# Summing the edge masks through four column quarters of the tensor engine, joined one row later, in a three-layer graph network kernel

## The reference, cut to what matters

```python
for l in range(N_LAYERS):                       # 3
    f1 = relu(x[row] @ nb_W[l] + nb_b[l]); f2 = relu(x[col] @ self_W[l] + self_b[l])
    h = relu(concatenate([f1, f2], axis=1) @ att1_W[l] + att1_b[l])
    log_alpha = (h @ att2_W[l] + att2_b[l])[:, 0]
    mask = clip(sigmoid(log_alpha) * (ZETA - GAMMA) + GAMMA, 0.0, 1.0)
    rowsum = segment_sum(mask, row, num_segments=n) + 1e-06
    d_inv_sqrt = clip(rowsum ** (-0.5), 0.0, 10.0)
    vals = mask * d_inv_sqrt[row] * d_inv_sqrt[col]
    x = segment_sum(vals[:, None] * x[col], row, num_segments=n)
    out = out + x
```

## Time and profile before

| what | before |
|---|---|
| median of 3 runs | 4434.0 us (4422.53, 4434.0, 4437.3) |
| the profiled execution's own time | 4420.38 us |
| its span in the profile | 4418.5 us |
| tensor engine matmul busy | 3818.8 us (86%) |
| tensor engine weight loads busy | 3641.2 us (82%) |
| vector engine busy | 3743.0 us (85%) |
| scalar engine busy | 1965.6 us (44%) |
| GpSimd busy | 2440.8 us (55%) |
| mean granted clock of the tensor engine | 0.947 of full speed |
| mask stage of layer 1, first to last matmul of the mask sums | 1350.7 to 1829.2 us |
| the same of layer 2 | 2392.9 to 2873.2 us |
| the same of layer 3 | 3437.9 to 3918.0 us |

### The profile page before, as it was taken

The page is one execution under the profiler, slowest core; times in us unless marked ns, Lnnn a source line. Parts: engine busy times, 40 slices in busy tenths (PEclk is TensorE's granted clock), DMA queues, the critical chain, the costliest instruction groups (busy, mean ns, idle before and its releaser), DMA issues. The chain is left out here.

```text
span 4418.5 us, 256510 instructions
## 1 busy us (share of the span) xinstructions
PE 3818.8 (86%) x99277; PEld 3641.2 (82%) x99278; DVE 3743.0 (85%) x5930; ACT 1965.6 (44%) x4794; POOL 2440.8 (55%) x3237
## 2 busy tenths in 40 slices
PE   5888577877859999799988999979997999979997
PEld 4777477777739999788886999979886999978887
DVE  8999878888867888799995888789996788879998
ACT  5888466776731212255552121145553112125554
POOL 3655377777831222388982222279885122238887
PEclk8888799999979999899998999989998999989999
DMA  1000099999926777566653777656662677756665
GB/s 30 2 2 2 17 268 285 294 286 283 287 68 233 243 243 244 165 171 171 171 141 128 242 244 242 215 156 171 170 171 82 222 243 244 243 159 171 172 171 138
DMA packets 533726, 794.14 MB, mean 180 GB/s; under 512 B 67990, under 2 KB 467786, under 8 KB 533642
## 3 DMA queue, kind: packets, MB, share of 16 engines
q1 hardware_dynamic: 500714, 714.25, 51.3%
q0 software_dynamic: 32928, 78.72, 8.3%
HBM read 672.34 MB, written 120.42 MB: 179 GB/s over the span
## 5 line engine op out<-in xcount | busy, mean ns | idle before, releaser
L1370 POOL TENSOR_TENSOR message<-message 128x448 f32<-128x448 f32 x1029 | 1242.4, 1239 | 211.1 <-ACT message L1354 211.1
L1141 PE MATMUL pre_ps<-rows_a,hotT_a 128*128 128x64 bf16 x21609 | 1289.8, 194 | 45.2 <-DMA hotT_a<-hot_scratch 27.9
L1141 PE MATMUL pre_ps<-table,hotT_a 128*128 128x64 bf16 x21609 | 1290.6, 194 | 7.1 <-issue 6.9
L1141 PEld LDWEIGHTS pre_ps<-rows_a,hotT_a 128*128 128x128 fp8e4 x21609 | 1132.2, 98 | 52.7 <-issue 52.3
L1141 PEld LDWEIGHTS pre_ps<-table,hotT_a 128*128 128x128 fp8e4 x21609 | 1132.9, 98 | 8.0 <-issue 8.0
L1381 DVE TENSOR_TENSOR message<-message 128x448 f32<-128x448 f32 x1029 | 993.7, 966 | 69.3 <-POOL message L1370 69.3
L1221 DVE SCALAR_TENSOR_TENSOR weighed<-pre_ps,w 128x448 f32<-128x448 f32 x1029 | 643.1, 625 | 311.0 <-PE pre_ps L1141 219.2
L1354 ACT ACTIVATE message<-high_ps,mask 128x64 f32<-128x64 f32 x3087 | 699.8, 327 | 295.2 <-PE high_ps L1313 276.5
L1325 PE MATMUL sum_ps<-message,hot_b 128*128 128x192 bf16 x7203 | 783.9, 247 | 6.3 <-DVE message L1381 5.7
L1313 PE MATMUL low_ps<-table,hot_b 128*128 128x64 bf16 x12348 | 531.5, 193 | 160.6 <-DMA hot_b<-hot_scratch 65.3
L1189 POOL TENSOR_SCALAR fresh<-gate 128x49 f32<-128x49 f32 x147 | 35.3, 240 | 1114.8 <-ACT gate L1169 1114.8
(11 more groups left out here) (150 smaller groups left out, 4988.0 us busy)
## 6 DMA issues: line engine op xcount, KB each, us to landing
hotT_a<-hot_scratch SPq DMA_DIRECT2D x1029, 224.0 KB, 4.5
hot_b<-hot_scratch SPq DMA_DIRECT2D x1029, 224.0 KB, 2.8
hot_scratch<-hot SPq DMA_DIRECT2D x343, 336.0 KB, 10.3
hot_a<-hot_scratch SPq DMA_DIRECT2D x147, 784.0 KB, 5.1
places<-slots_scratch POOLq DMA_DIRECT2D x686, 112.0 KB, 6.8
out<-res SPq DMA_DIRECT2D x1, 1536.0 KB
slots_scratch<-bins SPq DMA_DIRECT2D x49, 16.0 KB, 1.4
raw<-in_src SPq DMA_DIRECT2D x1, 768.0 KB
```

The costliest lines, as they stand in the source:

```text
L1141: last = nc.tensor.matmul(pre_ps[g][:, j, :], hotT[:, b, g, end, j * P:(j + 1) * P].bitcast(FP8), table, start=end + part == 0, stop=end = ...
L1370: pool.tensor_tensor(message[:, g, :, 1, :], message[:, g, :, 0, :], top[:, g, :, 0, :, 1], ALU.subtract).then_inc(s["rest_ready"], 1)
```

## The change

The roles of the two operands in the mask sums are swapped, and the 49 bins are dealt out over four column tiles of the array. The three parts of a bin's masks become the stationary operand (3 columns, at column 0, 32, 64 or 96 by the bin's number modulo 4) and the one-hot matrix becomes the moving one (128 columns). So each quarter of `total_ps[:, 0:128]` holds, in three of its partitions, sums over a quarter of the bins. The scalar engine copies the 128 x 128 result out twice (bf16 and f32), GpSimd splits it into three bf16 parts (three operations), and in the next row three matmuls with a column of ones add all partitions up into `total_ps[:, 128:129]`, after group 1. The vector engine copies this column out after group 2, in place of the reduction at the row's end. The mask sums stand after group 4 in place of group 5. The scalar engine now makes the gates first, copies the table rows of the next row after them, and then waits for the mask sums. The table gets a 50th, zeroed block so that this copy may run one row past the end. The sync engine waits for the mask sums (`quartered`) in place of `summed`. After the last row come one join, the last mask sums, their copy and split, and one more join.

```diff
-    SUMS_AT = max(0, NG - 2)
+    SUMS_AT = max(0, NG - 3)
+    ADD_AT = min(1, SUMS_AT)
@@ sync engine
-                    wait_count(sp, s, s["summed"], r + 1)
+                    wait_count(sp, s, s["quartered"], r + 1)
@@ tensor engine
                     pe.wait_ge(s["parts_ready"], r + 1)
-                    pe.wait_ge(s["taken"], r + 1)
+                    pe.wait_ge(s["taken"], r + 2)
...
-                            last = nc.tensor.matmul(total_ps[:, 0:PARTS], hot[:, b, g, j * P:(j + 1) * P].bitcast(FP8),
-                                                    parts[:, t, :], start=t == 0, stop=t == NB - 1)
+                            at = 32 * (t % 4)
+                            last = nc.tensor.matmul(total_ps[at:at + PARTS, 0:P], parts[:, t, :],
+                                                    hot[:, b, g, j * P:(j + 1) * P].bitcast(FP8), start=t < 4,
+                                                    stop=t >= NB - 4, tile_position=(0, at), skip_group_check=True)
+                    last.then_inc(s["quartered"], 1)
+
+                def add_quarters(next_but_one):
+                    pe.wait_ge(s["quarters_ready"], next_but_one)
+                    pe.wait_ge(s["taken"], next_but_one)
+                    hold_waits(pe, s)
+                    for part in range(PARTS):
+                        last = nc.tensor.matmul(total_ps[:, P:P + 1], quarter_parts[:, part, :], unit[:, :],
+                                                start=part == 0, stop=part == PARTS - 1)
                     last.then_inc(s["summed"], 1)
...
                         gather(r * NG + g, r, g, b, nth)
+                        if g == ADD_AT and not first:
+                            add_quarters(r)
                         if g == SUMS_AT and not first:
                             sum_masks(r - 1, 1 - b, nth if b == 1 else nth - 1)
                 each_row(pe, NB, row)
+                add_quarters(NB)
                 sum_masks(NB - 1, 0, NB // 2 + 1)
+                add_quarters(NB + 1)
@@ scalar engine
+                def take_quarters(r):
+                    act.wait_ge(s["quartered"], r + 3)
+                    act.wait_ge(s["summed"], r + 1)
+                    nc.scalar.activation(quarter_parts[:, 0, :], total_ps[:, 0:P], ACT.Copy)
+                    nc.scalar.activation(quarters[:, :], total_ps[:, 0:P], ACT.Copy).then_inc(s["quarters_taken"], 1)
...
                 def row(r, b, nth, first):
-                    if not first:
-                        act.wait_ge(s["gathered"], r * NG)
-                    nc.scalar.activation(rows[:, b, :].rearrange("p (a d) -> p a d", d=D),
-                                         k.table_s[:, bass.ds(r, 1), :, :].rearrange("p r a d -> p (r a) d"),
-                                         ACT.Copy).then_inc(s["rows_ready"], 1)
-                    if not first:
+                    if first:
+                        fetch_rows(0, 0)
+                        fetch_rows(1, 1)
+                    else:
                         gates(r - 1, 1 - b)
+                        act.wait_ge(s["gathered"], (r + 1) * NG)
+                        fetch_rows(r + 1, 1 - b)
+                        take_quarters(r - 1)
                 each_row(act, NB, row)
                 gates(NB - 1, 0)
+                take_quarters(NB - 1)
@@ GpSimd
                     pool.sem_inc(s["parts_ready"], 1)
+                    wait_count(pool, s, s["quarters_taken"], r + 1)
+                    step(pool.tensor_tensor(quarters[:, :], quarters[:, :], quarter_parts[:, 0, :], ALU.subtract))
+                    step(pool.tensor_copy(quarter_parts[:, 1, :], quarters[:, :]))
+                    step(pool.tensor_tensor(quarter_parts[:, 2, :], quarters[:, :], quarter_parts[:, 1, :], ALU.subtract))
+                    pool.sem_inc(s["quarters_ready"], 1)
@@ vector engine
                 dve.sem_inc(s["weigh"], NG)
-                dve.sem_inc(s["taken"], 1)
+                dve.memset(unit[:, :], 1.0)
+                dve.memset(quarter_parts[:, :, :], 0.0).then_inc(s["quarters_ready"], 1)
+                dve.memset(total_ps[:, 0:P], 0.0).then_inc(s["taken"], 1)
...
-                def take(r, b):
-                    dve.wait_ge(s["summed"], r + 3)
-                    dve.tensor_reduce(k.sums[:, bass.ds(r, 1)], total_ps[:, 0:PARTS], X, ALU.add).then_inc(s["taken"], 1)
+                def take(next_but_one):
+                    dve.wait_ge(s["summed"], next_but_one)
+                    dve.tensor_copy(k.sums_from[:, bass.ds(next_but_one - 1, 1)], total_ps[:, P:P + 1])\
+                        .then_inc(s["taken"], 1)
...
-                    if not first:
-                        take(r - 1, 1 - b)
+                        if g == ADD_AT + 1 and not first:
+                            take(r)
```

More of the change, by code:

```diff
@@ L146, in allocate @@
     k.one, k.two = k.both[:, :, 0:k.D], k.both[:, :, k.D:2 * k.D]
-    k.table = sb("table", [P, k.NB, PARTS, 2 * k.D], BF16)
+    k.table_all = sb("table", [P, k.NB + 1, PARTS, 2 * k.D], BF16)
+    k.table = k.table_all[:, 0:k.NB, :, :]
     k.table_s, k.table_d = k.table[:, :, :, 0:k.D], k.table[:, :, :, k.D:2 * k.D]
@@ L193, in _ @@
             nc.vector.memset(k.onesb[:, :], 1.0)
+            nc.vector.memset(k.table_all[:, k.NB, :, :], 0.0)
             nc.vector.tensor_copy(k.number[:, :], k.iota[:, :])
@@ L937, in allocate_layers @@
     k.mask = sb("mask", [P, k.NB * k.NB], F32)
-    k.sums = sb("sums", [P, k.NB], F32)
+    k.sums_from = sb("sums", [P, k.NB + 1], F32)
+    k.sums = k.sums_from[:, 1:k.NB + 1]
 def node_products(nc, k, l, w):
@@ L1104, in edge_masks @@
         pre_ps = [ps(f"pre_ps{g}", [P, 8, D]) for g in range(NG)]
+        quarters = sb("quarters", [P, P], F32)
+        quarter_parts = sb("quarter_parts", [P, PARTS, P], BF16)
+        unit = sb("unit", [P, 1], BF16)
         total_ps = ps("total_ps", [P, 512])
         sems = " ".join([f"in{b}_{g}" for b in range(2) for g in range(NG)] + ["src_in0", "src_in1"])
-        with phase(nc, "passed rows_ready gathered weigh logits gated parts_ready summed taken step pool_step "
+        with phase(nc, "passed rows_ready gathered weigh logits gated parts_ready quartered quarters_taken quarters_ready summed taken "
+                       "pool_step "
                        + sems, again=True) as (s, block):
@@ L1126, in _ @@
             def _(pe):
-                pe.sem_inc(s["summed"], 2)
+                pe.sem_inc(s["quartered"], 2)
                 pe.sem_inc(s["gathered"], NG)
@@ L1170, in gates, with fetch_rows @@
                         .then_inc(s["gated"], 1)
+                def fetch_rows(r, b):
+                    nc.scalar.activation(rows[:, b, :].rearrange("p (a d) -> p a d", d=D),
+                                         k.table_all[:, bass.ds(r, 1), :, 0:D].rearrange("p r a d -> p (r a) d"),
+                                         ACT.Copy).then_inc(s["rows_ready"], 1)
                 def row(r, b, nth, first):
-                    if not first:
-                        act.wait_ge(s["gathered"], r * NG)
-                    nc.scalar.activation(rows[:, b, :].rearrange("p (a d) -> p a d", d=D),
-                                         k.table_s[:, bass.ds(r, 1), :, :].rearrange("p r a d -> p (r a) d"),
-                                         ACT.Copy).then_inc(s["rows_ready"], 1)
-                    if not first:
+                    if first:
+                        fetch_rows(0, 0)
+                        fetch_rows(1, 1)
+                    else:
                         gates(r - 1, 1 - b)
+                        act.wait_ge(s["gathered"], (r + 1) * NG)
+                        fetch_rows(r + 1, 1 - b)
+                        take_quarters(r - 1)
                 each_row(act, NB, row)
                 gates(NB - 1, 0)
+                take_quarters(NB - 1)
             @block.gpsimd
@@ L1227, in row @@
                             reduce(q - 1, NG - 1, 1 - b)
-                    if not first:
-                        take(r - 1, 1 - b)
+                        if g == ADD_AT + 1 and not first:
+                            take(r)
                 each_row(dve, NB, row)
                 reduce(NB * NG - 1, NG - 1, 0)
-                take(NB - 1, 0)
-                dve.wait_ge(s["taken"], NB + 1)
+                take(NB)
+                take(NB + 1)
+                dve.wait_ge(s["taken"], NB + 2)
 def scale_rows(nc, k):
```

## The result

| what | before | after |
|---|---|---|
| median | 4432.4 us (7 runs) | 4408.4 us (7 runs) |
| ratio of after to before | | 0.9945, 95% interval 0.9932 to 0.9958 |
| on another chip, with more runs of before | 4404.2 us (11 runs) | 4381.3 us (6 runs), ratio 0.9944 (0.9931 to 0.9957) |
| span of the profiled execution | 4418.5 us | 4392.3 us |

What follows compares the result with a forecast made beforehand. The mask stage was taken as bound by TensorE's issue. 144 rows at -0.28 us (-1.24 + 0.66 + 0.22 + 0.08) gave -40, tails +7: -33 from 4434, so 4401 us, range 4368 to 4492.

Steps and rivals of the forecast that it cites:

- the likeliest case: Mask-sum burst: column tiles overlap and switches are cheap; 4401 us, 4368 to 4415 by the switches' cost, chance 0.45.
- Removed: Mask stage on TensorE: the old burst of 49 mask sums goes away, 1.24 us a row.
- The burst: Mask sums on TensorE: 49 matmuls in four overlapping column tiles, 0.0135 us apart, add 0.66 us a row.
- the rival's mechanism: Mask-sum burst: 0.025 us is a fixed time per matmul, so the burst keeps 1.24 us; 4485 us, chance 0.30.
- The switches: Changes of tile shape into and out of the burst: 0.11 us each, 0.22 a row; 0.375 with a full drain.
- The join: Next row on TensorE: three matmuls of 128 stationary columns add 0.076 us a row, with no wait for data.
- The thin margin: Mask sums one group earlier: parts ready 0.16 us before the burst, cost nothing; each 0.1 us late costs 14 us.
- Scalar engine, GpSimd, sync engine: Added copies, split and moved waits in the loop: hidden, zero cost; copies 0.55 us a row without cover.
- Tails: End of each of three mask stages: unhidden copies, split and join add 2.4 us each, 7 us together.

Runs made afterwards that it cites:

- The run that takes the tails out: The changed kernel with the last row's masks summed in the old form (128 columns stationary, three moving, one reduction): 4372.4 us, ratio to before 0.9924.

## Why the prediction was right, point by point

The direction and the likeliest case (4368 to 4415) held; by its own steps:

1. Removed, 1.24 us a row: as read.
2. The burst: forecast 0.66 at 0.0135, measured 0.69 at 0.0140. The reason given was only half right. It left open whether the old 0.0253 was the load of 128 columns or a fixed time and leaned on the change altering both. The runs with 32 moving columns settle it: the fixed time is real (0.0251 in one tile with a load of 3 columns), so the rival's mechanism exists, but it holds for a tile and not for the engine (0.0070 over four tiles). Of the two things altered the tiles did it and the load did not: with the load altered and one tile the kernel takes 283 us more than before.
3. The switches: forecast 0.22 as twice the 0.11 of rows with another kind of tiling, measured 0.23 as 0.09 and 0.14. That the sum agrees to 0.01 is in part luck, for the way out is no fixed price. From the start of the burst's last matmul to the next gather are 0.152 us after 128 moving columns, with one, two or four tiles (latency 0.219); after 32 columns 0.109 with one tile and 0.185 with four (latency 0.176). By the rule of the Trainium skill ("TensorEngine Tiling (Array Packing)", Key Properties) that a change of mode drains the engine, the two switches would be 0.375, as an estimate from the rows' latencies. That did not come in the changed kernel, but in the run with four tiles and 32 columns the last matmul's time had run out before the next one started.
4. The join: 0.08 as forecast, with no wait.
5. The thin margin: forecast 0.16, found 0.2 to 0.3 by the timeline, and the run one group earlier gives the same. No idle before the burst is put down to GpSimd.
6. Scalar engine, GpSimd, sync engine: nothing, as forecast. Where the table rows are copied doesn't matter to the time, by experiment. What the sync engine's earlier release does was not tried by itself.
7. Tails: forecast 2.4 us each, measured 2.46, and this is luck: two terms were off and made up for each other. The burst was to save 0.4 us and costs 0.10 more (1.55 instead of 1.45), since the clock is at its lower level there and the four tiles are then 0.0257 apart; the prediction used the distance of the loop. The copies and the split, with the waits ahead of them, were to take 2.45 and take 1.95 (1811.58 to 1813.53). Wait and join are 0.41 for 0.38. The run that takes the tails out gains 8.9 for the 7.4.

A row is 0.24 us shorter in the steady part (19.91 to 19.43 for two), against a forecast of 0.28: 144 rows give -34, the tails +7, together -27. The loss of 0.04 a row is the distance of 0.0140 (0.03) and the switches (0.01). The measured 24 have an interval of 19 to 30, so the 27 are not contradicted. By the profiles the three mask stages, from the last table write to the last sum, are 8.8, 8.6 and 6.7 us shorter, 24.0 in all; the other 2.2 of the 26.2 us of span lie outside them. At 9 us a stage, layers 1 and 2 have what the steps give, and the 2 us that are missing are in layer 3, in its first rows. TensorE stands still there with nothing that the profile names, in both kernels but in other places, and after some of these stops the granted clock is at its lower level. Two of them in layer 3 after the change, and below them the clock of the stretches that follow:

```profile
3411.52 0.23 PE L1149 MATMUL pre_ps<-rows_a,hotT_a 128*128 128x64 bf16 x1 [2.88 <-issue]
...
3426.85 0.25 PE L1149 MATMUL pre_ps<-rows_a,hotT_a 128*128 128x64 bf16 x3 [1.86 <-issue]
...
3411.00:3417.00 6.00, 5.48 (x105) 5.48 (x106) 2.28 (x5) 0.00 (x0) 1.49 (x6) 0.50 0.19 69
...
3428.00:3431.00 3.00, 3.00 (x61) 3.00 (x59) 1.59 (x4) 0.00 (x0) 0.41 (x2) 0.50 0.22 78
```

Apart from the stage's first gathers, which are at the lower level in both kernels, the clock is at 0.50 for 10.2 us of layer 3 after the change, and for 6.8 us before. This scatters between executions of the same kernel: from the first gather to the last sum the three stages after the change take 494.2, 494.6 and 497.1 us in one profile and 496.3, 494.5 and 495.4 in the other. Why TensorE stops there was not tried and stays open.

## What to carry to other kernels

Where many matmuls with few output rows stand in a row, the array's column tiles, taken in turn, divide both the streaming and, nearly, the fixed time per matmul by their number; placing them in runs of one tile loses most of that. Count the price around it first: two changes of tiling (0.23 us here) and whatever must join the tiles. A pipeline that is free inside a loop is paid in full where the loop ends, so the last pass may be worth another form (9 us here). What is bound by streaming is slower at the lower clock, and a burst that stands behind a wait of 5 us meets it.

## What was not expected of the hardware

- A load of 96 stationary columns spaces matmuls 0.045 us apart, one of 128 not more than 0.025.
- In the run with 96 columns the clock falls although TensorE has no idle, in about every third row. After the burst of 1504.18 to 1506.39 the granted clock (third column from the right) goes to half and back:

```profile
1504.00:1506.00 2.00, 2.00 (x53) 2.00 (x50) 1.70 (x4) 0.00 (x0) 0.00 (x0) 1.00 0.18 65
...
1507.00:1508.00 1.00, 1.00 (x29) 1.00 (x26) 0.00 (x0) 0.00 (x0) 0.00 (x0) 0.62 0.00 0
1508.00:1510.00 2.00, 2.00 (x42) 2.00 (x39) 1.22 (x3) 0.00 (x0) 0.00 (x0) 0.50 0.88 219
...
1511.00:1513.00 2.00, 2.00 (x75) 2.00 (x72) 1.69 (x4) 0.59 (x2) 0.64 (x3) 1.00 1.06 384
```

  At 0.50 (1.2 GHz) 42 matmuls touch 2 us, at 1.00 (2.4 GHz) 75. That row takes 12.3 us instead of 9.95, 1.4 us more than its longer burst accounts for. Some 50 rows are like it, which makes 70 of the remaining 87 us. In the loops of the kernels before and after, with bursts of 1.24 and 0.69 us, the clock stays at 1.00.
- In runs of one tile, only the last four matmuls of a tile run beside the first four of the next.
